# A macaron block on one core: flag 2's bank and place, tile 2's norm, the loads, the orders and one warm-up product changed

## The chip, the cores and the metric

The kernel runs on one core of one Trainium2 chip. The metric is device microseconds of one execution, as the median of several; three runs of the kernel before gave 368.39, 368.41 and 369.13 us. The engines are TensorE (PE, matrix products into PSUM), VectorE (DVE), ScalarE (ACT), GpSimd (POOL) and SyncE (SP), which here only issues DMAs. Each engine runs its own instructions in order and waits on semaphores for the others.

## The reference

The input is 16 x 256 tokens of 128 features. A feed-forward block, an attention-like block with cumulative sums, and the same feed-forward block again are added to it, each behind a layer norm:

```python
def _L0_ffn_ref(x, w1_w, w1_s, w2_w, w2_s, h1_w, h1_s, h2_w, h2_s, w3_w, w3_s):
    h = silu(_tlin(x, w1_w, w1_s)) * _tlin(x, w2_w, w2_s)     # 128 -> 512
    h = gelu(_tlin(h, h1_w, h1_s))                            # 512 -> 512
    h = gelu(_tlin(h, h2_w, h2_s))                            # 512 -> 512
    return _tlin(h, w3_w, w3_s)                               # 512 -> 128

def _L0_attn_ref(...):
    h = layer_norm(x, gamma, beta)
    keys = h @ Wk.T + bk;  values = h @ Wv.T + bv;  key_att = keys @ Wka.T + bka
    w = exp(key_att / sqrt(128));  w = w / cumsum(w, axis=1)
    return cumsum(w * keys, axis=1) * values

x = x + 0.5 * ffn(layernorm(x));  x = x + attn(layernorm(x));  x = x + 0.5 * ffn(layernorm(x))
```

`_tlin(x, w, s)` is a product with a matrix of -1, 0 and 1, scaled by `s`.

## The kernel before

The 4096 tokens are eight tiles of 512. Each goes through the first feed-forward pass as tile 0 to 7, through attention (`a0` to `a7`) and through the second pass as tile 8 to 15. Activations stand transposed, features on partitions. Every activation is split into a high part (`act_hi`, cast to fp32r) and a low part (`act_lo`, the rest), so that two fast products per weight block replace one slow one.

One tile of the feed-forward pass is `p1.0` to `p1.3` (first layer, gate and up, four blocks of four products), `p2.0` to `p2.3` and `p3.0` to `p3.3` (second and third layer, eight products each) and `p4` (eight products). ACT does `tanh`, `gelu` and the high parts (`high1`, `high2`, `high3`), DVE `gate`, `up`, the low parts (`low1` to `low3`) and the final addition `dt`. The orders are written out by hand: `START` (lines 27 to 42) for the time before the loop, `SECOND_LAYER` (45 to 49) for tile 0's second layer, and `STEPS` (50 to 185), one string per engine and step. In a string, `p2.1` is block 1 of the tile due at this step, `2:t` the stage `t` of tile 2, `a0:u` of attention tile 0. `t` is the split of the normalised input into `xn_hi` (ACT) and `xn_lo` (DVE).

There are two ways for a tile's norm. The first three tiles (`BY_PE`, line 188) are normalised in rows: DVE takes statistics (`stats`, `aggr`, `veps`), POOL makes `rstd` and `nmr`, ACT writes `z`, PE transposes it (`t`, lines 787 to 798). All other tiles go over POOL: it aggregates the statistics (`aggregate`, 534 to 553), SP parks mean and root in DRAM (`park`, 488 to 495, rows<-pair) and loads them back widened over all partitions (`wide`, 497 to 504, wide<-rows), and POOL adds and multiplies (`xn.0`, `xn.1`, lines 555 to 573) on the transposed input `xt_sb`.

The weights are proved to fit the fast format while the kernel runs: their low bits are reduced to a flag (`bits:...`, `flag:raise`), PE sums it over the partitions into one PSUM element (`flag:sum`, line 751), DVE casts it (`flag:copy`, 1024), and PE loads it into a register and branches to the fast or the general program (lines 854 to 860). There are three such flags and branches: flag 1 ahead of tile 0's first layer, flag 2 ahead of its second layer, flag 3 ahead of all the rest. Flag 2 is summed in `y_ps`, which `p1.3` of tile 0 writes later, so `p1.3` waits for the flag (line 682). Flag 3 is summed in `xt_ps`.

SP's loads (471 to 486) are in one queue: weights and tile 1 first, then, once `w3` and `h2` are down, all of `x` from tile 2 on (1536 KB), four attention weights and all of `xt` (2048 KB). Before its first real product PE multiplies ones (`warm_up`, 842): four products at once, two after the first variance, one after `rstd`.

## Time and profile before

| | us |
| --- | --- |
| median of three runs | 368.41 |
| profiled execution, its own time | 368.15 |
| its span, first to last instruction | 366.4 |
| PE busy | 359.3 |
| DVE busy | 316.2 |
| ACT busy | 283.1 |
| POOL busy | 163.3 |

What follows is read from one profiled execution. Times in it count from the span's start. PE's matrix products overlap: a product of 512 columns is shown with 0.39 us, while the next one starts 0.23 us after it, so the distance between starts is what counts.

### The profile page before, as it was taken

Reading aid. Unit: us, or ns where it says so; the run is one execution under the profiler, and the core shown is the slowest. Engines: PE = TensorE matmul, PEld = TensorE weight load, DVE = VectorE, ACT = ScalarE, POOL = GpSimd, SP = SyncE. Lnnn points to the kernel's source line nnn. Section 1 sums busy time; section 2 is a strip of 40 time slices with the busy share of each in tenths; the row PEclk is TensorE's granted clock in tenths of the full one; section 3 lists DMA queues with packets and bytes.
Section 4 is the critical chain, followed back from the end, with each engine's and each line's share of the span. In section 5 each row is a group of like instructions: output and inputs, shape, how many; then the busy total and the mean of one; then the engine's idle time right before and its main releaser. Section 6 shows DMA issues by size and latency. Waiting matters only on the chain.

```text
span 366.4 us, 5194 instructions
## 1 busy us (share of the span) xinstructions
PE 359.3 (98%) x1578; PEld 285.1 (78%) x1578; DVE 316.2 (86%) x550; ACT 283.1 (77%) x465; POOL 163.3 (45%) x251
## 2 busy tenths in 40 slices
PE   7999999999999999999999999999999999999996
PEld 2678888787877777788778787787778777888885
DVE  5999688999989998889899989998899799857642
ACT  4998777987777879776887968877897697686763
POOL 3553344649045565812685545652573740530000
PEclk9999999999999999999999999999999999999999
DMA  7770103030100301300222012012022020040001
GB/s 245 270 294 4 54 3 107 8 110 9 58 2 0 86 29 36 83 0 2 59 59 59 1 59 59 0 59 86 0 59 88 2 86 2 4 111 2 1 30 63
DMA packets 16256, 20.94 MB, mean 57 GB/s; under 512 B 7008, under 2 KB 8288, under 8 KB 15968
## 3 DMA queue, kind: packets, MB, share of 16 engines
q1 hardware_dynamic: 15504, 19.75, 18.2%
q10 hardware_dynamic: 720, 0.80, 0.7%
q8 instruction: 16, 0.26, 0.3%
q14 instruction: 16, 0.13, 0.1%
HBM read 18.36 MB, written 2.18 MB: 56 GB/s over the span
## 4 chain that ended last, share of the span: by engine, by line
PE 96%; DVE 2%; issue 1%; ACT 1%; POOL 0%; POOLq 0%; ACTq 0%
PE hid_ps L643 62%; PE gate_ps L643 8%; PE y_ps L643 8%; PE up_ps L643 7%; PE y_ps L662 2%; PE xt_ps L829 2%; PE xt_ps L833 2%; PE xt_ps L836 2%; PE y_ps L843 1%; PE gate_ps L707 1%; PE up_ps L707 1%; DVE gate L1070 0%; PE xt_ps L643 0%; DVE xt_sb L1142 0%; PE xt_ps L656 0%
## 5 line engine op out<-in xcount | busy, mean ns | idle before, releaser
L643 PE MATMUL hid_ps<-act_hi,hi_h 128*128 128x512 f32 x480 | 193.3, 403 | 0.0
L643 PE MATMUL hid_ps<-act_lo,hi_h 128*128 128x512 f32 x480 | 186.7, 389 | 0.0
L1092 DVE TENSOR_TENSOR act_lo<-full,act_hi 128x512 fp32r<-128x512 f32 x185 | 132.8, 742 | 23.6 <-ACT act_hi L909 20.6
L902 ACT ACTIVATE full<-hid_ps,vec 128x512 f32<-128x512 f32 x123 | 84.1, 687 | 57.2 <-PE hid_ps L643 51.7
L643 PEld LDWEIGHTS hid_ps<-act_hi,hi_h 128*128 128x128 f32 x480 | 90.3, 188 | 22.8 <-issue 2.6
L643 PEld LDWEIGHTS hid_ps<-act_lo,hi_h 128*128 128x128 f32 x480 | 90.2, 188 | 21.3 <-issue 2.6
L909 ACT ACTIVATE act_hi<-full 128x512 fp32r<-128x512 f32 x127 | 78.6, 628 | 1.6
L567 POOL TENSOR_TENSOR xnt<-xt_sb,wide 128x512 f32<-128x512 f32 x21 | 29.4, 1400 | 45.8 <-DMA wide<-rows 45.8
L885 ACT ACTIVATE tanh<-gate_ps,s_half 128x512 f32<-128x512 f32 x60 | 40.4, 680 | 7.4 <-PE gate_ps L643 7.3
L1070 DVE SCALAR_TENSOR_TENSOR gate<-tanh,gate_ps 128x512 f32<-128x512 f32 x60 | 40.3, 674 | 6.5 <-ACT tanh L885 6.4
L1082 DVE SCALAR_TENSOR_TENSOR full<-up_ps,s_half,gate 128x512 f32<-128x512 f32 x60 | 44.1, 741 | 1.1
L890 ACT ACTIVATE act_hi<-full 128x512 fp32r<-128x512 f32 x60 | 36.9, 625 | 1.9 <-DVE full L1082 1.7
L573 POOL TENSOR_TENSOR xnt<-xnt,wide 128x512 f32<-128x512 f32 x21 | 30.0, 1428 | 3.2 <-POOL xnt L567 0.4
L622 POOL TENSOR_TENSOR xt_sb<-xt_sb,adelta 128x512 f32<-128x512 f32 x8 | 12.3, 1532 | 42.7 <-DVE adelta L1174 42.7
L540 POOL TENSOR_TENSOR pair_diff<-stats 128x4 f32<-128x4 f32 x21 | 8.2, 388 | 44.2 <-DVE stats L1040 44.2
L1158 DVE RECIPROCAL rcsum<-csum 128x256 f32<-128x256 f32 x16 | 27.8, 1740 | 0.0
L553 POOL TENSOR_TENSOR pair<-veps,half 128x4 f32<-128x4 f32 x21 | 26.1, 1244 | 3.3 <-POOL veps L550 0.4
L643 PE MATMUL gate_ps<-xn_hi,hi_w 128*128 128x512 f32 x59 | 25.1, 425 | 0.3 <-ACT full L902 0.3
L643 PE MATMUL y_ps<-act_hi,hi_w 128*128 128x512 f32 x60 | 23.8, 396 | 0.0
L643 PE MATMUL y_ps<-act_lo,hi_w 128*128 128x512 f32 x60 | 23.4, 390 | 0.0
L643 PE MATMUL gate_ps<-xn_lo,hi_w 128*128 128x512 f32 x59 | 23.0, 391 | 0.0
L643 PE MATMUL up_ps<-xn_hi,hi_w 128*128 128x512 f32 x59 | 23.0, 390 | 0.0
(170 smaller groups left out, 440.3 us busy)
## 6 DMA issues: line engine op xcount, KB each, us to landing
wide<-rows SPq DMA_DIRECT2D x42, 256.0 KB, 3.7
xt_sb<-xt SPq DMA_DIRECT2D x1, 2048.0 KB, 10.6
out<-xt_sb SPq DMA_DIRECT2D x7, 256.0 KB, 4.0
x_sb<-x SPq DMA_DIRECT2D x1, 1536.0 KB, 6.8
raw_h<-h2t SPq DMA_DIRECT2D x4, 256.0 KB, 7.1
raw_h<-h1t SPq DMA_DIRECT2D x2, 256.0 KB, 6.1
rows<-pair SPq DMA_DIRECT2D x21, 4.0 KB, 2.2
raw_w<-w2t ACTq DMA_DIRECT2D x1, 256.0 KB, 4.0
```

The lines of the kernel that those rows point to most:

```text
L553: eng.tensor_tensor(pair_b[q][:, 1, :], veps[:, :], half[:, :], ALU.pow).then_inc(s_pow, 1)
L567: eng.tensor_tensor(xnt_b[i][:, :], xt_tile(t), wide_b[i][:, 0:TOK], ALU.add).then_inc(s_centred, 1)
L573: eng.tensor_tensor(xnt_b[i][:, :], xnt_b[i][:, :], wide_b[i][:, TOK:2 * TOK], ALU.mult).then_inc(s_xn, 1)
L643: mm = eng.matmul(ps, w, a, start=(first and n == 0), stop=(last and n == len(seq_) - 1))
L885: eng.activation(tanh_b[m % 2][:, :], gate_home(T, m)[:, :], ACT.Tanh, scale=s1_half[:, m:m + 1]).then_inc(s_tanh, 1)
L890: eng.activation(act_hi[first_act(T)][:, m, :], full1[m % 2][:, :], ACT.Copy).then_inc(s_hi[1], 1)
L902: eng.activation(full23[m % 2][:, :], home23(n, T, m)[:, :], ACT.Gelu, scale=col("sh1" if n == 2 else "sh2", m)).then_inc(s_gelu[n], 1)
L909: eng.activation(act_hi[n][:, m, :], full23[m % 2][:, :], ACT.Copy).then_inc(s_hi[n], 1)
L1070: eng.scalar_tensor_tensor(gate_b[m % 2][:, :], tanh_b[m % 2][:, :], 1.0, gate_home(T, m)[:, :], ALU.add, ALU.mult).then_inc(s_gate, 1)
L1082: eng.scalar_tensor_tensor(full1[m % 2][:, :], up_home(T, m)[:, :], s12_half[:, m:m + 1], gate_b[m % 2][:, :], ALU.mult, ALU.mult).then_in ...
L1092: eng.tensor_tensor(act_lo[a][:, m, :], full[m % 2][:, :], act_hi[a][:, m, :].bitcast(F32), ALU.subtract).then_inc(s_lo[n], 1)
L1158: eng.reciprocal(rcsum[:, b], csum[:, b]).then_inc(s_rc, 1)
```

## The change

- `WARM_UP` loses its last product, the one that waited for `rstd`.
- Flag 2 is summed in `gate_ps[0]` after `p1.3` of tile 0, and waits for the first `gate` to have read that bank; `p1.3` no longer waits for the flag.
- Tile 2's norm goes over POOL, with `stats_2` before tile 0's last `low1`. It gets loads of its own: tile 2 of `x` and of `xt`, ahead of the other tiles. The rest of `xt` is two loads.
- All orders are written anew.

```diff
-WARM_UP = (4, 2, 1)
+WARM_UP = (4, 2)
 START:
-        "p1.0 p1.1 flag:sum2 p1.2 p1.3",
+        "p1.0 p1.1 p1.2 p1.3 flag:sum2",
...
-    "p2ahi.0 p2ahi.1 p2ahi.2 p2ahi.3 p2alo.1 p2alo.3 p2bhi.3 p2alo.0 p2alo.2 p2bhi.0 p2bhi.2 t p2blo.0 p2bhi.1 "
+    "p2ahi.2 p2ahi.1 p2ahi.3 p2alo.2 p2alo.3 p2alo.1 p2ahi.0 p2bhi.0 p2bhi.1 p2bhi.2 p2alo.0 p2blo.1 p2blo.0 "
...
 STEPS["PE"], first two rows:
-        "p1.2 p1.3 fold p3.0 p3.1",
-        "t 0:p3.2 p1.0 0:p3.3 p2.0 p1.1 p2.1 p2.2 p2.3 p4 p1.2 p1.3 a0:u p3.0 p3.1 p3.2 p3.3",
+        "p1.2 fold p1.3 p3.0 p3.1 p3.2 p3.3",
+        "p1.0 p1.1 p2.0 p2.1 p4 p2.2 p2.3 p1.2 a0:u p1.3 p3.0 p3.1 p3.2 p3.3",
...
-BY_PE = (0, 1, 2)
-AGGREGATE = 3
+BY_PE = (0, 1)
+AGGREGATE = 2
...
-            return (hid_ps[0], y_ps, xt_ps)[part - 1][0:1, 0:1]
+            return (hid_ps[0], gate_ps[0], xt_ps)[part - 1][0:1, 0:1]
...
-            xload(2, NT, s_xr)
+            xload(2, 3, s_x2t)
+            eng.dma_start(xt_tile(2), xt[:, 2 * TOK:3 * TOK]).then_inc(s_xt2, 16)
+            xload(3, NT, s_xr)
...
-            eng.dma_start(xt_sb[:, :], xt).then_inc(s_xt, 16)
+            eng.dma_start(xt_sb[:, 0:2 * TOK], xt[:, 0:2 * TOK]).then_inc(s_xt, 16)
+            eng.dma_start(xt_sb[:, 3 * TOK:], xt[:, 3 * TOK:]).then_inc(s_xt, 16)
...
+                elif t == 2:
+                    eng.wait_ge(s_xt2, 16)
                 elif t < NT:
-                    eng.wait_ge(s_xt, 16)
+                    eng.wait_ge(s_xt, 32)
...
-                if (T, m) in ((0, 3), (1, 1)):
-                    eng.wait_ge(s_flag, T + 2)
+                if (T, m) == (1, 1):
+                    eng.wait_ge(s_flag, 3)
...
                 if part == 2:
-                    eng.wait_ge(s_xlo_half, 2)
+                    eng.wait_ge(s_gate, 1)
```

PE, tile 0's first layer and flag 2 (`inexact` is the flag, `hi_w1` and `hi_w2` the gate's and the up's weights). Before:

```order
L643 MATMUL up_ps1<-xn_lo,hi_w2 128x512
L764 MATMUL y_ps<-ones,inexact 1x1 [waits s_xlo_half,s_inexact]
L643 MATMUL hid_ps0<-xn_hi,hi_w1 128x512
L643 MATMUL hid_ps0<-xn_lo,hi_w1 128x512
L643 MATMUL hid_ps1<-xn_hi,hi_w2 128x512
L643 MATMUL hid_ps1<-xn_lo,hi_w2 128x512
L643 MATMUL y_ps<-xn_hi,hi_w1 128x512 [waits s_flag]
```

The same place on PE after the change:

```order
L649 MATMUL up_ps1<-xn_lo,hi_w2 128x512
L649 MATMUL hid_ps0<-xn_hi,hi_w1 128x512
L649 MATMUL hid_ps0<-xn_lo,hi_w1 128x512
L649 MATMUL hid_ps1<-xn_hi,hi_w2 128x512
L649 MATMUL hid_ps1<-xn_lo,hi_w2 128x512
L649 MATMUL y_ps<-xn_hi,hi_w1 128x512
L649 MATMUL y_ps<-xn_lo,hi_w1 128x512
L649 MATMUL xt_ps<-xn_hi,hi_w2 128x512
L649 MATMUL xt_ps<-xn_lo,hi_w2 128x512
L770 MATMUL gate_ps0<-ones,inexact 1x1 [waits s_gate,s_inexact]
```

The flag's sum moved behind all products of the first layer, and none of these waits for the flag any more.

DVE, from flag 1's cast to the second `up` (`full1_1`), before:

```order
L1027 CAST flag_i<-hid_ps0 1x1 [waits s_fps]
L1012 TENSOR_REDUCE bits<-raw_h1 128x1 [waits s_h1_0]
L1122 TENSOR_TENSOR xn_lo<-xt_ps,xn_hi 128x256 [waits s_xhi_half]
...
L1022 TENSOR_REDUCE inexact<-bits 128x1 [waits s_bits_w2,s_bits_w1,s_bits_h1]
L1045 MEMSET fence 128x1 [waits s_bn]
L1047 BN_AGGR mv<-stats_1 128x2 x4
L1070 SCALAR_TENSOR_TENSOR gate_0<-tanh_0,gate_ps0 128x512 [waits s_tanh]
L1054 TENSOR_SCALAR neg_mean<-mv 128x4 [waits s_nmr,s_mv]
L1055 TENSOR_SCALAR veps<-mv 128x4
L1027 CAST flag_i<-y_ps 1x1 [waits s_fps]
L1082 SCALAR_TENSOR_TENSOR full1_0<-up_ps0,s12_half,gate_0 128x512 [waits s_p1,s_gate,s_scaled]
L1070 SCALAR_TENSOR_TENSOR gate_1<-tanh_1,gate_ps1 128x512 [waits s_tanh]
```

DVE, the same place after:

```order
L1124 TENSOR_TENSOR xn_lo<-y_ps,xn_hi 128x256 [waits s_xhi_half]
L1014 TENSOR_REDUCE bits<-raw_h1 128x1 [waits s_h1_0]
...
L1072 SCALAR_TENSOR_TENSOR gate_0<-tanh_0,gate_ps0 128x512 [waits s_tanh]
L1042 BN_STATS stats_1<-x_sb 128x6 [waits s_x1t]
L1042 BN_STATS stats_1<-x_sb 128x6 x3
L1084 SCALAR_TENSOR_TENSOR full1_0<-up_ps0,s12_half,gate_0 128x512 [waits s_p1,s_gate,s_scaled]
L1047 MEMSET fence 128x1 [waits s_bn]
L1049 BN_AGGR mv<-stats_1 128x2 x4
L1024 TENSOR_REDUCE inexact<-bits 128x1 [waits s_bits_w2,s_bits_w1,s_bits_h1]
L1072 SCALAR_TENSOR_TENSOR gate_1<-tanh_1,gate_ps1 128x512 [waits s_tanh]
L1029 CAST flag_i<-gate_ps0 1x1 [waits s_fps]
```

The reduction of `h1`'s first part moved behind `xn_lo`, and flag 2's cast behind the second gate.

SP, its queue after the first loads: the last load of `x`, the attention weights, `xt`, and tile 3's and then attention tile 0's parked rows, before:

```order
L470 DMA x_sb<-x 128x3072 [waits s_w3,s_h2_3]
L485 DMA wk<-wkt 128x128
...
L486 DMA xt_sb<-xt 128x4096
L495 DMA rows<-pair_0 128x2x4 [waits s_pow]
L503 DMA wide_0<-rows 128x512 [waits s_parked_0]
```

SP after the change, where `pair_0` is tile 2's:

```order
L473 DMA x_sb<-x 128x512 [waits s_w3,s_h2_3]
L487 DMA xt_sb<-xt 128x512
L473 DMA x_sb<-x 128x2560
L490 DMA wk<-wkt 128x128
...
L491 DMA xt_sb<-xt 128x1024
L492 DMA xt_sb<-xt 128x2560
L501 DMA rows<-pair_0 128x2x4 [waits s_pow]
L509 DMA wide_0<-rows 128x512 [waits s_parked_0]
```

The loads are cut so that tile 2 comes first, and tile 2's parked rows now follow the last piece of `xt` in the same queue.

## Rows read from the trace of the kernel before

**Rows 1.** Busy time by stretch: PE, PEld, DVE, ACT, POOL; clock, DMA share, GB/s.
```profile
27.00:360.00 333.00, 332.99 (x1457) 267.77 (x1458) 292.77 (x479) 261.31 (x421) 150.08 (x226) 1.00 0.15 40
```
**Rows 2.** Timeline of PE, 30 to 34 us: start, us, what.
```profile
30.63 0.60 PE L656 MATMUL xt_ps<-ident,z 128*128 128x128 f32 x4
...
31.30 0.39 PE L643 MATMUL hid_ps<-act_lo,hi_h 128*128 128x512 f32 x1
...
33.14 0.39 PE L643 MATMUL gate_ps<-xn_lo,hi_w 128*128 128x512 f32 x1
```
**Rows 3.** Chain that ended last, in order of time: start, us, what.
```profile
56.26 7.25 PE hid_ps L643 x32
```
**Rows 4.** Timeline, the start, PE and DVE; last, the line of the flag's loads.
```profile
2.12 3.15 PE L843 MATMUL y_ps<-ones 128*1 128x256 f32 x7 [2.12 <-POOL ident L530]
...
6.65 0.81 PE L843 MATMUL y_ps<-ones 128*1 128x256 f32 x3
...
7.30 0.24 PE L756 MATMUL hid_ps<-ones,bits 128*1 128x1 f32 x4
...
7.58 0.15 DVE L1027 CAST flag_i<-hid_ps 1x1 int32<-1x1 f32 x1 [0.30 <-PE hid_ps L756]
...
8.69 0.36 PE L678 MATMUL gate_ps<-xn_hi,hi_w 128*128 128x256 f32 x1 [0.56 <-ACT xn_hi L968]
...
L856 PEldq TENSOR_LOAD <-flag_i x3: 304/307/492, 7.8 to 22.8; - x3
```
**Rows 5.** Timeline, 6 to 14 us, DVE, and PE's first product of the second layer.
```profile
7.65 0.67 DVE L1012 TENSOR_REDUCE bits<-raw_h 128x1 f32<-128x512 uint16 x1
...
8.70 0.41 DVE L1122 TENSOR_TENSOR xn_lo<-y_ps,xn_hi 128x256 fp32r<-128x256 f32 x1
...
12.04 0.14 DVE L1027 CAST flag_i<-y_ps 1x1 int32<-1x1 f32 x1
...
13.46 0.75 DVE L1082 SCALAR_TENSOR_TENSOR full<-up_ps,s_half,gate 128x512 f32<-128x512 f32 x1
...
13.64 0.47 PE L707 MATMUL gate_ps<-act_hi,hi_h 128*128 128x512 f32 x1 [0.22 <-ACT act_hi L890]
```
**Rows 6.** Timeline of PE, 20 to 28 us: third stage's first product, and `p3.0`.
```profile
24.12 0.39 PE L643 MATMUL gate_ps<-xn_hi,hi_w 128*128 128x512 f32 x1
...
26.86 0.49 PE L643 MATMUL hid_ps<-act_hi,hi_h 128*128 128x512 f32 x1
```
**Rows 7.** Timeline of POOL, 12 to 45 us: casts of `h2`, tile 3's norm.
```profile
18.27 2.76 POOL L584 CAST hi_h<-raw_h 128x512 fp32r<-128x512 f32 x4
...
30.02 0.21 POOL L540 TENSOR_TENSOR pair_diff<-stats 128x4 f32<-128x4 f32 x1 [4.71 <-DVE stats L1040]
...
38.73 1.29 POOL L567 TENSOR_TENSOR xnt<-xt_sb,wide 128x512 f32<-128x512 f32 x1 [5.62 <-DMA wide<-rows]
40.17 1.56 POOL L573 TENSOR_TENSOR xnt<-xnt,wide 128x512 f32<-128x512 f32 x1
```
**Rows 8.** Timeline of SP's issues, 13 to 40 us: start and time of issuing.
```profile
16.05 0.45 SPq L486 DMA_DIRECT2D xt_sb<-xt  x1
...
34.73 0.34 SPq L503 DMA_DIRECT2D wide<-rows  x1
```
**Rows 9.** Lines of tiles `xn_hi` and `wide`: min/median/max in ns; last, landing in us.
```profile
L961 ACT ACTIVATE xn_hi<-xnt x13: 616/626/642, 50.5 to 328.7; 128x512 fp32r<-128x512 f32 x13
...
L1127 DVE TENSOR_TENSOR xn_lo<-xnt,xn_hi x13: 675/683/1124, 51.4 to 329.3; 128x512 fp32r<-128x512 f32 x13
...
DMA to landing us min/median/max: 3.1/3.7/4.8
```
**Rows 10.** DMA issues from 13 to 36 us: KB each, median us to landing.
```profile
xt_sb<-xt SPq DMA_DIRECT2D x1, 2048.0 KB, 10.6
...
wk<-wkt SPq DMA_DIRECT2D x1, 64.0 KB, 6.0
...
rows<-pair SPq DMA_DIRECT2D x1, 4.0 KB, 1.6
```

62 lines of the change are left out of this document (27 added, 35 removed), and 178 rows, old and new, of tables (SECOND_LAYER, START, STEPS).

## The prediction

> **What bounds the kernel now.** First the table of stretches: from 27 us to 360 us PE (TensorE) is busy for 332.99 of 333 us, at a granted clock of 1.00, with VectorE (DVE) busy for 293 us and ScalarE (ACT) for 261 [rows 1]. There the time is PE's own work, and no other engine's saving is worth anything. What an order can give or lose lies in the first 35 us, where PE is still fed by single results. After 360 us the last tile's chain runs; its PE order is the same in the changed kernel, so I count nothing for it. The sum is therefore the time at which one fixed point of PE's stream is reached, before and after; all behind it moves along. I take the low product of tile 2's first gate (`p1.0` of tile 2), with the whole of tile 0's third layer done. Before, that product starts at 33.14 [rows 2], with `0:p3.3` (8 products) still to come; 32 products take 7.25 in the steady stream, 0.227 each [rows 3]. So the point lies at 33.14 + 8 x 0.227 = 34.95.
>
> **Start, to the first product.** One warm-up product goes. It is two passes; three passes span 6.65 to 7.30, 0.22 each [rows 4], so the flag sum behind it starts 0.43 sooner, at 6.87. Its inputs are there (DVE's reductions of `w1`, `w2` end before 6.41, where `z` begins). DVE's flag cast then waits for the three `z` pieces instead of PE and starts near 7.2 instead of 7.58 [rows 4], so PE's first product comes at about 8.3 instead of 8.69. The transposes move by the same 0.43, and so do ACT's `xn_hi` and DVE's `xn_lo`: the second `xn_lo` starts at 8.27 instead of 8.70 [rows 5].
>
> **Flag 2.** Before, PE's sum of flag 2 stands between `p1.1` and `p1.2` and makes them wait for DVE. That stall goes: all products of tile 0's first layer run through and end near 12.2. But the second branch needs the flag itself. On DVE, from the second `xn_lo` (8.70) to the second `up` (13.46) lie 4.76 us without a gap [rows 5]. The same instructions stand there in the new order plus `bits:h1.0`, 0.67 [rows 5], which before filled the wait between the flag cast and `xn_lo` and now comes behind it. So the second `up` starts at 8.27 + 4.76 + 0.67 = 13.70, and the flag cast, which now has only the two small operations of `veps` between itself and that `up`, at about 13.45, ending at 13.6. Before, the cast ended at 12.18 [rows 5]. From a cast's end to PE's first product took 0.96 for flag 1 (7.73 to 8.69, `TENSOR_LOAD` and branch within it) [rows 4]; a part of this may be the wait for `xn_hi`, so 0.96 is the upper bound and 0.5, the longest load of the flag alone (492 ns) [rows 4], the lower. I take 0.85, nearest to the one whole passage seen. The second layer then begins at 13.6 + 0.85 = 14.45 instead of 13.64 [rows 5]: **+0.8**, with PE idle some 2.2 us before it, and the first `act_hi` is no later than that by my count of ACT (about 13.9).
>
> **Second stage.** Before it ran from 13.64 to 24.12 [rows 5, 6], 10.48 for 40 products of 0.23, four transposes (0.44) and a flag sum (0.2): 9.85 of work and 0.6 of waits. In the new order each operand is ready before its turn, since PE comes later to the same chain; I leave 0.1 for waits. End: 14.45 + 9.95 = 24.4, **+0.3**. The third flag is ready about 0.5 before PE's last four products there, so its branch is hidden as it is now, where the stream goes on at 24.12 without a pause.
>
> **Third stage to `p3.0`.** Before: 24.12 to 26.86 [rows 6], 2.74 for 8 products (1.82) and the four short ones of `fold`, the rest a wait for the fourth `gelu2`. Now `fold` stands ahead of `p1.3`, and it writes `xt_ps`, which DVE's `1:gate.1` must have read; that gate starts only after `flag:copy3`, `up.0`, `low2.0`, `low2.1`, near 25.05, and ends near 25.7. `p1.3` then waits a little for the fourth `gelu2`. I get 27.2 for `p3.0`: **+0.35**, bounds +0.0 and +0.8.
>
> **Tile 2's transposes** leave PE. They cost 31.30 - 30.63 - 0.23 = **-0.44** [rows 2]. Then 32 products of `p3` and the high product: 27.2 + 33 x 0.227 = 34.7. Against 34.95 that is -0.25: PE alone would gain a quarter of a microsecond.
>
> **Tile 2's norm on GpSimd (POOL).** This is the new wait. The pieces, as tile 3 has them now: the aggregation from 30.02 [rows 7] to the parking's issue, 34.73 - 1.6 = 33.13; the parking 1.6 [rows 8, 10]; the widening to the first addition 38.73 - 34.73 = 4.0; addition and multiplication 38.73 to 41.73 = 3.0 [rows 7, 8]; then `xn_hi` on ACT 0.63 and `xn_lo` on DVE 0.68 [rows 9]. POOL starts it after `low1` and three casts of `h2`: before, the casts began at 18.27 and all four took 2.76 [rows 7]; now the first comes at about 18.35 and the norm at 20.5, and the roots are done at 23.6. Parked at once, the rows would be back at 25.2. But the queue on SyncE (SP) is full: the load of `xt`, issued at 16.05, lands after 10.6, at 26.65 [rows 8, 10]. Does it hold the parking? `wk`, 64 KB, issued right behind the 1536 KB of `x`, took 6.0, while the pair of 256 KB each on an idle queue took 4.0 and the 4 KB of the parking 1.6 [rows 7, 8, 10]. So yes: I take 26.65 (the bounds are 25.2 and 27.5). Then 4.0 + 3.0 gives 33.65, 0.63 + 0.68 and some 0.15 of hand-over 35.1. The cost of the split loads themselves is nothing: the same bytes, three more issues.
>
> The Trainium skill, page "DMA: Bandwidth & Descriptors", section "Queues, rings and completion order", says that each DMA engine consumes a ring in order and that a semaphore's increment lands only after every earlier write of that engine. By this rule the parking can't be told done before the last piece of `xt` is down, which speaks against the change; the trace agrees with it (6.0 for `wk`). Without the rule the sum would be that of the first rival.
>
> **Sum.** The point is reached at the later of 34.7 (PE) and 35.1 (tile 2's normalised rows): 35.1 against 34.95, **+0.15**. `2:t` stands on DVE ahead of `1:up.3`, which `p1.1` needs: ready at 35.8, PE there at 35.8, nothing. On ACT `2:t` holds `gelu3.2`, which `p2.0` needs at 36.7 and has at 35.6. The rest has the same work; tile 3's rows, next in the chain, are ready near 46 and wanted near 48. The profiled execution took 368.15 (span 366.4), 0.26 below the median: 368.3 there, 368.55 for the median; I say **368.5**. A measurement here can tell about 0.2% (0.74 us) from no change.
>
> **The rivals.** (1) *The loads don't hold the parking*: it lands at 25.2, the rows are ready at 33.7, PE decides: -0.25, 368.15. Against it stands `wk`. (2) *Clearly faster*: as (1), and DVE's `bits:h1.0` costs nothing and the third stage has no new wait (0.35 less): -0.25 - 0.67 - 0.35 = -1.3, 367.1; half of it 367.6. For it speaks that my hand count of DVE has some 0.3 of play at each step. (3) *Slower, by the norm's chain*: the mechanism is PE waiting at `p1.0` of tile 2. It decides from 34.7 on and makes the kernel measurably slower once the rows come after 35.7. The widening's transfers took up to 4.8 where I have 4.0 [rows 9], and the queue may end at 27.5: 0.8 + 0.85 = 1.65 at worst, rows at 36.75 and +1.8, 370.2; the middle of this case is rows at 36.2, +1.25: 369.65. (4) *Slower, by the clock*: The warm-up passes are spaced 0.42 (six from 2.12 to 4.63) and later 0.22 [rows 4], that is the level of 1.2 and of 2.4 GHz, though the granted clock reads 1.00 throughout. The new stop of 2.2 us before the second layer is longer than any in PE's stream before. If the clock falls there, the slow passes at the start, some 4.2 us from 2.12 on [rows 4], are the nearest price: half of them lost, 2.1, less the 0.4 of slack: +1.85, 370.25. The Trainium skill, page "TensorE: Matmul & The Clock Gate", Part 1, has the clock halved when PE has been idle; whether this stop is enough no row here shows. (5) *A new wait in the steady stretch*: DVE's 88% [rows 1] leaves little play for the new orders: +0.3 to +1.
>
> **Chances.** Forecast 0.41; (1) 0.17; (2) 0.19; (3) 0.12; (4) 0.05; (5) 0.06. Within 0.2%: 0.41 + 0.17 = 0.58, less 0.01 for a small (5) that I count as slower: 0.57. Faster by over 0.2%: 0.19. Slower: 0.24. The range from 367.4 to 369.9 leaves out the better half of (2), 0.09, and the worst of (3) and (4), 0.09.
>
> **What would show it.** PE's second layer begins at 14.45, not 13.64; flag 2's cast is at 13.4; `p3.0` at 27.2; no transposes of tile 2 on PE; POOL's first `xnt` at about 30.7; PE waits about 0.4 before tile 2's low gate product, released by `xn_hi` and `xn_lo`; no other wait until 360. The prediction is wrong if the second layer starts before 14 (the DVE count), if the parked rows land before 26 (the queue), or if PE's products after 14 us are spaced 0.43 apart (the clock).

## The result, and the profile after

The changed kernel takes 369.72 us in the median of 20 executions (368.65 to 373.43); the kernel before, timed beside it, 368.46. The ratio is 1.004, with a 95% interval of 1.0029 to 1.0051 (the quotient of the two medians is 1.0034; the ratios given here and below are not exactly these quotients): the change makes the kernel slower by 0.4%, 1.26 us in the medians. The forecast was 368.5 and no measurable change; the time lies in its range, but the kernel did become slower. Two executions far above all others, 518.52 us of the kernel before here and 402.87 us of `b_nowarm2` below, count in no ratio and in none of the counts below. The profiled execution of the changed kernel took 369.33 us, its span is 367.5 us.

The points of the prediction in the two profiled executions (us from the span's start; the two rows marked * are starts of products, read below or in the rows of before; 34.95 is the prediction's sum, not a row):

| | before | forecast | after |
| --- | --- | --- | --- |
| first product of the first layer | 8.69 | 8.3 | 8.62 |
| cast of flag 2 | 12.04 | 13.45 | 13.62 |
| first product of the second layer | 13.64 | 14.45 | 14.40 |
| third stage, first product | 24.12 | 24.4 | 24.58 |
| `p3.0` of tile 0 | 26.86 | 27.2 | 27.30 |
| parked rows of tile 2 are down | - | 26.65 | 27.46 |
| fixed point, low product of tile 2's first gate * | 34.95 | 35.1 | 35.40 |
| first of the last four products * | 361.82 | 361.97 | 363.36 |

PE's timeline of the changed kernel from the start to `p3.0` (start, us, what; in brackets the idle time before it and its releaser), to be held against [rows 4, 5, 6]:

```profile
3.77 3.62 PE L847 MATMUL y_ps<-ones 128*1 128x256 f32 x8
7.19 0.28 PE L762 MATMUL hid_ps<-ones,bits 128*1 128x1 f32 x4
...
8.62 0.36 PE L684 MATMUL gate_ps<-xn_hi,hi_w 128*128 128x256 f32 x1 [0.45 <-ACT xn_hi L970]
...
12.23 0.39 PE L649 MATMUL xt_ps<-xn_lo,hi_w 128*128 128x512 f32 x1
13.16 0.19 PE L770 MATMUL gate_ps<-ones,inexact 128*1 128x1 f32 x2 [0.55 <-DVE inexact L1024]
14.40 0.47 PE L713 MATMUL gate_ps<-act_hi,hi_h 128*128 128x512 f32 x1 [1.04 <-ACT act_hi L892]
...
27.30 0.39 PE L649 MATMUL hid_ps<-act_hi,hi_h 128*128 128x512 f32 x1
```

Eight warm-up passes take 3.42 us from 3.77 to the flag sum at 7.19, 0.43 each to the last, where before the last three were spaced 0.22. So without the product the flag sum begins 0.11 us sooner (7.30 before) and not 0.43. All products of the first layer run through to 12.62, and then PE stands for 1.78 us, but for the flag's sum.

ACT and DVE in the stop, the same execution, show what it waited for:

```profile
12.20 0.64 ACT L916 ACTIVATE csum<-raw_h 128x512 f32<-128x512 uint16 x1
12.80 0.63 ACT L916 ACTIVATE rcsum<-raw_h 128x512 f32<-128x512 uint16 x1
...
13.42 0.63 ACT L892 ACTIVATE act_hi<-full 128x512 fp32r<-128x512 f32 x1
```
```profile
12.95 0.16 DVE L1024 TENSOR_REDUCE inexact<-bits 128x1 f32<-128x6 f32 x1
13.03 0.68 DVE L1072 SCALAR_TENSOR_TENSOR gate<-tanh,gate_ps 128x512 f32<-128x512 f32 x1
13.62 0.14 DVE L1029 CAST flag_i<-gate_ps 1x1 int32<-1x1 f32 x1
```

ACT's pass over `h1.3` (`csum` is only its scratch output) and the read of its sum end at 12.92. DVE's reduction to flag 2 (`inexact`) begins right behind them, and the pass over `h2.0` keeps the first `act_hi` until 13.42. The second layer needs both, the flag and `act_hi`.

POOL, SP and PE on tile 2's norm, which has no counterpart before ([rows 7 to 10] show tile 3's):

```profile
30.67 1.67 POOL L575 TENSOR_TENSOR xnt<-xt_sb,wide 128x512 f32<-128x512 f32 x1 [6.76 <-DMA wide<-rows]
32.49 1.29 POOL L581 TENSOR_TENSOR xnt<-xnt,wide 128x512 f32<-128x512 f32 x1
```
```profile
23.37 0.39 SPq L501 DMA_DIRECT2D rows<-pair  x1
27.48 0.34 SPq L509 DMA_DIRECT2D wide<-rows  x1
```
```profile
34.65 0.47 PE L649 MATMUL gate_ps<-xn_hi,hi_w 128*128 128x512 f32 x1
35.40 0.50 PE L649 MATMUL gate_ps<-xn_lo,hi_w 128*128 128x512 f32 x1 [0.28 <-DVE xn_lo L1129]
35.73 0.40 PE L649 MATMUL up_ps<-xn_hi,hi_w 128*128 128x512 f32 x1
```

POOL's norm begins at 20.69. The parking, issued at 23.37, is down at 27.46, 0.18 us behind the last load of `xt`. That load was issued at 16.85 (before, at 16.05, with fewer loads ahead of it) and was down 10.4 us later.

PE's wait is the one that was forecast, a little longer: its distances there are 0.32, 0.75 and 0.33 where 0.23 is normal. Behind it the prediction had PE's stream unchanged. It is not. The table of stretches (us, busy time and instructions of PE, PEld, DVE, ACT, POOL; clock, DMA share, GB/s) shows three stretches in which PE is not full, where [rows 1] had 0.01 us of idle time in all:

```profile
34.00:60.00 26.00, 25.72 (x115) 20.80 (x114) 21.84 (x42) 20.47 (x35) 14.88 (x28) 1.00 0.16 42
...
135.00:138.00 3.00, 2.95 (x13) 1.81 (x12) 2.42 (x4) 2.33 (x5) 1.07 (x1) 1.00 0.00 0
...
331.00:334.00 3.00, 2.85 (x13) 2.05 (x12) 2.02 (x4) 1.48 (x3) 0.12 (x1) 1.00 0.00 0
```

Between 60 and 135 and between 138 and 331 us PE is full. The busy time hides most of a wait, since the product ahead of it is shown with 0.39 us; the distances between starts tell it. At 136 us two distances exceed 0.227 by 0.21 and 0.11, at 332 us by 0.31 and 0.11. The first of the last four products (L747 before, L753 after), one line of each kernel's timeline:

```profile
361.82 0.60 PE L747 MATMUL gate_ps<-full,raw_w 128*128 128x256 f32 x2
```
```profile
363.36 0.60 PE L753 MATMUL gate_ps<-full,raw_w 128*128 128x256 f32 x2
```

So 1.54 us are lost up to there: 0.45 at the fixed point and 0.11 behind it (35.40 to 35.73), 0.32 at 136 us, 0.42 at 332 us, and 0.24 in small differences all along. Some 0.2 of these 0.24 belong to the new steps and not to a wait: `a_best` and its two filled variants below have the same steps and no wait of this kind, and still need 327.06, 327.00 and 327.17 us from the fixed point to these products, where the kernel before needs 326.87. (The span is 1.1 longer and not 1.5, because the last stores of this execution landed 0.4 sooner after their issue, in 2.1 us and not 2.5.)

### The profile page after: what moved, and what is told of

Same layout as the page of the kernel before. It is cut to its first block, busy times and chain, and to the rows that moved or that the text cites. A ratio compares the mean times of both kernels' runs of the same rounds, so it can differ in the third digit from the quotient of the medians.

```text
span 367.5 us, 5188 instructions
## 1 busy us (share of the span) xinstructions
PE 359.6 (98%) x1572; PEld 284.8 (77%) x1572; DVE 316.2 (86%) x543; ACT 281.7 (77%) x461; POOL 171.7 (47%) x259
## 4 chain that ended last, share of the span: by engine, by line
PE 84%; DVE 4%; DMA 4%; POOL 4%; issue 2%; ACT 1%; POOLq 0%; ACTq 0%; DVEq 0%; SPq 0%
PE hid_ps L649 54%; PE gate_ps L649 7%; PE y_ps L649 7%; PE up_ps L649 7%; PE y_ps L668 2%; DMA wide<-rows 2%; DMA rows<-pair 2%; PE xt_ps L833 2%; PE xt_ps L840 2%; PE xt_ps L837 2%; PE y_ps L847 1%; POOL xnt L575 1%; DVE act_lo L1094 1%; DVE gate L1072 1%; POOL hi_h L592 1%
## 5 line engine op out<-in xcount | busy, mean ns | idle before, releaser
L575 POOL TENSOR_TENSOR xnt<-xt_sb,wide 128x512 f32<-128x512 f32 x22 | 32.6, 1484 | 44.7 <-DMA wide<-rows 44.7
L581 POOL TENSOR_TENSOR xnt<-xnt,wide 128x512 f32<-128x512 f32 x22 | 31.0, 1407 | 3.0 <-POOL xnt L575 0.4
L649 PE MATMUL gate_ps<-xn_hi,hi_w 128*128 128x512 f32 x59 | 26.0, 440 | 0.0
L649 PE MATMUL gate_ps<-xn_lo,hi_w 128*128 128x512 f32 x59 | 23.3, 394 | 0.4 <-DVE xn_lo L1129 0.3
L649 PE MATMUL y_ps<-act_hi,hi_w 128*128 128x512 f32 x60 | 23.3, 389 | 0.0
L649 PE MATMUL y_ps<-act_lo,hi_w 128*128 128x512 f32 x60 | 23.3, 389 | 0.0
L649 PE MATMUL up_ps<-xn_lo,hi_w 128*128 128x512 f32 x59 | 23.1, 391 | 0.0
## 6 DMA issues: line engine op xcount, KB each, us to landing
xt_sb<-xt SPq DMA_DIRECT2D x1, 1280.0 KB, 10.4
```

The costliest lines, as they stand in the source:

```text
L575: eng.tensor_tensor(xnt_b[i][:, :], xt_tile(t), wide_b[i][:, 0:TOK], ALU.add).then_inc(s_centred, 1)
L581: eng.tensor_tensor(xnt_b[i][:, :], xnt_b[i][:, :], wide_b[i][:, TOK:2 * TOK], ALU.mult).then_inc(s_xn, 1)
L649: mm = eng.matmul(ps, w, a, start=(first and n == 0), stop=(last and n == len(seq_) - 1))
```

## The experiments

All runs are compared with the kernel before, timed beside them on the same chip. To tell where time goes, each profiled execution is read at two places: the *fixed point*, and the *stretch* from it to the first of the last four products (326.87 before, 327.96 after). Both vary from one execution to the next: the changed kernel and five runs with its orders from the second stage on (`a_warm`, `a_busy`, `a_stop`, `a_stop2`, `a_stop_fill`) have stretches of 327.54 to 327.96, and where their clock stays full, the fixed point lies between 34.98 and 35.98. A difference of 0.4 us between two single profiles therefore shows nothing by itself; a wait that is always there or never does.

### Warm-up product put back

```diff
-WARM_UP = (4, 2)
+WARM_UP = (4, 2, 1)
```

> The changed kernel with the warm-up product of TensorE put back (waiting for the root, as before); all else stays changed. Theory A (the removed product costs and gives nothing that reaches the end): in the profile of the changed kernel the two passes that went did not bring the flag sum forward by 0.43 us, because the passes kept their 0.43 spacing up to 7.19. With the product back the first product of the first layer starts between 8.55 and 8.75 (8.63 without it), and the low product of tile 2's first gate stays at 35.3 to 35.5, since tile 2's norm on GpSimd decides it. Time within 0.2 us of the changed kernel. Rival (the missing product leaves TensorE at the low clock for longer and this is carried to the end): 0.4 us or more faster than the changed kernel, and everything behind 8.6 us earlier by as much.

369.70 us, ratio 1.0035 (1.0023 to 1.0048). The first product comes at 9.16, the fixed point at 35.25, the last products at 363.13. The time doesn't move, as theory A has it, but the first product was expected at 8.75 at the latest: the warm-up passes kept their wide distance, 0.42 or 0.43 us, up to 7.21 us here. PE, half a microsecond late from there on, comes to the fixed point without a wait; its lateness, and rows that are down 0.5 sooner here (26.97), have taken the place of the wait.

### The xt loads behind tile 2's widening

```diff
-            eng.dma_start(xt_sb[:, 0:2 * TOK], xt[:, 0:2 * TOK]).then_inc(s_xt, 16)
-            eng.dma_start(xt_sb[:, 3 * TOK:], xt[:, 3 * TOK:]).then_inc(s_xt, 16)
...
                     wide("ffn" if stage == "wide" else "att", t)
+                    if (stage, t) == ("wide", 2):
+                        eng.dma_start(xt_sb[:, 0:2 * TOK], xt[:, 0:2 * TOK]).then_inc(s_xt, 16)
+                        eng.dma_start(xt_sb[:, 3 * TOK:], xt[:, 3 * TOK:]).then_inc(s_xt, 16)
```

> The changed kernel, with the two loads of xt (tiles 0 and 1, and tiles 3 to 11) issued by SyncE behind tile 2's parking and widening instead of ahead of them. Theory A (these loads stand in the queue ahead of the parking and hold it): the parking, issued near 23.4, lands within 1.6 to 2.2 us, before 25.8 (27.46 in the changed kernel), GpSimd's first addition of tile 2 starts near 29 (30.67), and the low product of tile 2's first gate starts when TensorE gets there, at 34.8 instead of 35.40; the time falls by 0.6 us against the changed kernel, to about 369.1. Rival B (the parking waits for the load of x, which is still in the queue, or for something else than xt): it still lands after 26.5, and the time stays within 0.2 us. Rival C (the widening then shares its transfers with the xt loads and is late): the parking is early but the first addition is still after 30.

368.83 us, ratio 1.0019 (1.0005 to 1.0033). PE has no wait at the fixed point any more:

```profile
34.48 0.39 PE L650 MATMUL gate_ps<-xn_hi,hi_w 128*128 128x512 f32 x1
34.71 0.39 PE L650 MATMUL gate_ps<-xn_lo,hi_w 128*128 128x512 f32 x1
```

34.71 is the time at which the prediction had PE arrive (34.7), and the last products are 0.94 sooner. The time gains too: the nine executions with a full clock have a median of 368.80, the eight such executions of `a_warm` and `a_stores` on the same chip 369.55. But the parking itself, with nothing large ahead of it, still took 3.3 us, issued at 23.30:

```profile
26.67 0.34 SPq L507 DMA_DIRECT2D wide<-rows  x1
```

Theory A expected it down before 25.8. The DMA queues of this execution from 23.3 to 27.6 us (packets, MB, share of 16 engines) show what moved:

```profile
q1 hardware_dynamic: 272, 0.00, 3.8%
q8 instruction: 1, 0.02, 1.9%
```

One packet of instructions, 16 KB, went at 24.23 for 1.32 us; 240 of the parking's 256 packets of 16 bytes went in the microsecond from 24 us, the last 16 from 25.54 to 25.69, beginning as the instruction packet ends (25.55). `a_mend` and `a_mend_pool` (below) show the same: the last 16 packets begin within 0.02 us of the end of the instruction packet, and the parking takes 3.0 and 3.3 us. In `a_best` and its two filled variants the parking is issued by 22.93, the instruction packet goes only at 25.6 or later, and the parking takes 1.6 us in all three, as in [rows 10]. So the likely reading is that the last 16 packets stood behind the instructions on one of the 16 DMA engines; the trace doesn't name the engine of a packet, and no run was made to test it.

With the loads ahead of it, the parking landed 0.18 to 0.31 us behind the last load of `xt` in all nine profiled executions of that kind: the loads do hold it. But that load itself landed sooner or later, so the parking took 3.1 to 5.5 us there and 3.0 to 3.3 with the loads behind it; in `a_pool`, with the loads ahead, the rows were down as early as here (26.66) and PE had no wait either. So theory A is right in the mechanism; its 1.6 us without the loads is wrong, and the 0.8 us between 27.46 and 26.65 are those of two single executions.

### The last widening ahead of the stores

```diff
-        "park 9:store 10:store 11:store wide store",
+        "park wide 9:store 10:store 11:store store",
```

> The changed kernel, with SyncE's last widening issued ahead of the stores of tiles 9 to 11 instead of behind them. Theory A (the 0.42 us that TensorE waits near 332.3 come from these stores, which stand between the parking and the widening): the parking of the last norm lands 1.6 us after its issue (2.84 in the changed kernel), the widening's transfers take under 3.8 us (4.2), TensorE does not wait there, and the last store is issued 0.42 us sooner relative to the product of the same place at 320 us: time 0.4 us under the changed kernel, 369.3. Rival (DVE's statistics for that norm, which come 0.9 us later than in the kernel before, decide): a wait of more than 0.2 us stays there.

PE's wait at 332 us is gone: 332.25 and 332.48 are the starts of the high and the low product of tile 15's first gate. It is a wait that belongs to this order: between 0.11 and 0.73 us were lost there in all nine profiled executions with the three stores ahead of the widening, and at most 0.04 in the six with the widening ahead. The stretch is 327.58 instead of 327.96. SP's issues in the changed kernel and here:

```profile
321.29 0.37 SPq L501 DMA_DIRECT2D rows<-pair  x1
321.71 1.44 SPq L519 DMA_DIRECT2D out<-xt_sb  x3
324.18 0.33 SPq L509 DMA_DIRECT2D wide<-rows  x1
```
```profile
321.46 0.37 SPq L501 DMA_DIRECT2D rows<-pair  x1
324.09 0.32 SPq L509 DMA_DIRECT2D wide<-rows  x1
```

The parking itself was hardly quicker (2.63 us, 2.89 in the changed kernel, expected 1.6); what the stores held were mainly the widening's own 512 KB: from its issue to POOL's first addition 3.59 us instead of 4.20. The time, 370.02 us, ratio 1.0044 (1.0029 to 1.0059) from five executions, does not show the gain; 0.4 us is within what five executions leave open.

### The old start in the changed kernel

```diff
-        "p1.0 p1.1 p1.2 p1.3 flag:sum2",
+        "p1.0 p1.1 flag:sum2 p1.2 p1.3",
```

and the `START` strings of ACT and DVE and flag 2's bank of the kernel before.

> The changed kernel, with the start of the kernel before on TensorE, VectorE and ScalarE (flag 2 summed in its old bank between the second and the third product group of the first layer, the old order of casts and flag work); the second and third stage, GpSimd's norm of tile 2 and all later orders stay changed. Theory A (the start is hidden behind tile 2's norm on GpSimd): the second layer begins at 13.6 to 13.8 instead of 14.40 and the third layer 0.5 to 0.8 us sooner, but the low product of tile 2's first gate still starts at 35.3 to 35.5, with TensorE waiting about 1.2 us there; time within 0.2 us of the changed kernel. Rival (the later second layer is what reaches the end): 0.5 to 0.8 us faster than the changed kernel, 369.0 or less, and the low product starts before 35.0.

372.15 us, ratio 1.0101 (1.0084 to 1.0117): both expectations fail. The second layer begins at 13.31, but PE stands for 2.8 us in the third stage, and behind that stop the granted clock falls (0.70 from 27 to 29 us, 0.50 from 29 to 31). The trace names no releaser for the stop (`issue`); that it comes of mixing two orders is my reading.

```profile
26.89 0.47 PE L649 MATMUL gate_ps<-xn_hi,hi_w 128*128 128x512 f32 x1 [2.77 <-issue]
...
29.65 0.63 PE L649 MATMUL up_ps<-xn_hi,hi_w 128*128 128x512 f32 x1
30.08 0.63 PE L649 MATMUL up_ps<-xn_lo,hi_w 128*128 128x512 f32 x1
```

The run says nothing on whether the start is hidden. It gave the clue to the next question: a mean granted clock of 0.994 or 0.995 over the execution, in all four of its executions. With the start of before (the kernel before itself, and later `b_nowarm` and `b_flag`) no execution whose clock is on record read below 0.998; of the changed kernel 3 in 20 read 0.993 to 0.995, and these took 370.48, 370.89 and 373.43 us.

### Three mends together

The xt loads and the last widening as above, and on ACT:

```diff
-        gelu2.3 a2:t high1.0 high2.3 7:t
+        gelu2.3 a2:t high2.3 high1.0 7:t
```

> The changed kernel with three edits of its orders: the two xt loads behind tile 2's widening, the last widening ahead of the three stores, and on ScalarE the high part high2.3 of tile 5's second layer ahead of high1.0 (the low part that follows it on VectorE took 1.09 us beside GpSimd and ended 0.25 us late for TensorE at 136 us). Theory A (the three waits are what the change cost: 0.6 near 35 us, 0.3 near 136, 0.4 near 332): low product of tile 2's first gate at 34.7, no wait of TensorE over 0.1 near 136 and near 332, last four products from 361.8 to 362.1 (361.82 before, 363.36 changed), time 368.2 to 368.6, that is within 0.1% of the kernel before. Rival (a wait that goes comes back further on, since VectorE and ScalarE are the ones that are late): last four products not before 362.4, time 368.8 or more.

369.08 us, ratio 1.0006 (0.9993 to 1.0020). The fixed point is at 34.83, the wait at 332 us is gone, the one at 136 us is not (0.21 and 0.11, as in the changed kernel), and a new one of 0.54 stands at 260 us. The stretch is 328.03, no better than unmended, as the rival has it: waits come back further on. The time speaks for theory A all the same, within 0.1% of the kernel before, and the interval doesn't meet that of the change (from 1.0029 on). The profiled execution is slower than the median of the nine with a full clock (368.79). DVE's `act_lo` at 132.8 and 134.2 us take 1.34 and 1.61 us here, beside POOL's operations, and two at 259 and 260.5 us take 1.76 and 1.77, where the changed kernel, whose POOL began its pair 0.55 us earlier, had 0.75 and 1.36. Hence the next try, to move POOL's instruction (`a_pool`).

### Warm-up product taken out of the kernel before

```diff
-WARM_UP = (4, 2, 1)
+WARM_UP = (4, 2)
```

> The kernel before, without the last warm-up product of TensorE, and nothing else. In the pair changed kernel / changed kernel with the product back, the first product of the first layer came at 8.62 without it and at 9.16 with it. Theory A (the product delays the flag sum by its own passes, 0.43 to 0.85): first product 0.3 to 0.5 us sooner than 8.69, and the second layer and the end sooner by the same, since the kernel before has no wait on tile 2's norm that hides it: 368.0. Rival (the second layer is set by VectorE and ScalarE, and only the first product moves): the second layer stays at 13.5 to 13.7 and the time within 0.15 us of the kernel before.

> The kernel before without the last warm-up product again, to settle a difference of 0.26 us. Theory A (in the profiled execution everything from the first product on came 0.6 us sooner): ratio to the kernel before 0.998 to 0.9995, and with the earlier run beside it clearly below 1. Rival (the gain of the profiled execution was the moment at which the clock rose, which differs from one execution to the next): ratio 0.9995 to 1.0005.

368.58 us and 368.00 us, ratios 0.9993 (0.9983 to 1.0003) and 0.9991 (0.9982 to 1.0000). In the two profiled executions the second layer begins at 13.04 and at 14.09. That difference is not the product's: DVE began the statistics of the first tile of `x`, for which it had waited, at 3.91 and at 4.68, and the last four warm-up passes, spaced 0.21 in both, began at 5.53 and at 6.30. Both ratios point the same way, some 0.3 us, but neither interval excludes 1 clearly. It is the one part of the change that may gain, and no version was found that gains more.

### Flag 2's bank and place in the kernel before

```diff
-        "p1.0 p1.1 flag:sum2 p1.2 p1.3",
+        "p1.0 p1.1 p1.2 p1.3 flag:sum2",
-        ... aggr gate.0 veps flag:copy2 up.0 gate.1 ...
+        ... aggr gate.0 veps up.0 flag:copy2 gate.1 ...
-            return (hid_ps[0], y_ps, xt_ps)[part - 1][0:1, 0:1]
+            return (hid_ps[0], gate_ps[0], xt_ps)[part - 1][0:1, 0:1]
```

> The kernel before, with one part of the change alone: flag 2 is summed in the first gate bank behind the last product of tile 0's first layer, and its cast stands behind the first up on VectorE. Nothing else is changed. Theory A (the place of the sum costs only what lies between the cast and the branch): the cast is at 12.8, the second layer starts at 13.8 to 13.9 instead of 13.64, and third layer and end are within 0.2 us of the kernel before, so the 0.75 us by which the second layer is later in the changed kernel are not the bank but the new order on ScalarE, where the casts of h1.3 and h2.0 now stand between the tanh and the first act_hi. Rival (the bank is what costs): second layer at 14.2 or later, time 0.4 us or more above the kernel before.

368.70 us, ratio 1.0004 (0.9992 to 1.0015). From the first product of the first layer to that of the second it is 4.93 us (8.22 to 13.15), before 4.95, after 5.78. The bank costs nothing, not even the 0.2 that I expected; so the 0.8 must come from the new orders of ACT and DVE around it.

### The changed start in the kernel before

```diff
-        "t vec:s1 bits:h1.1 bits:h1.3 tanh.0 tanh.1 tanh.2 high1.0 tanh.3 high1.1 ... bits:h2.0 "
+        "tanh.0 tanh.1 bits:h1.1 tanh.2 bits:h1.3 bits:h2.0 high1.0 tanh.3 high1.1 ..."
```

and DVE's and PE's orders of the changed start.

> The kernel before with the changed kernel's start on TensorE, ScalarE and VectorE (flag 2 behind the first layer in the gate bank, the new order of tanh, casts, flag and act_hi up to the second layer); the warm-up product, tile 2's norm on TensorE and all later orders are those of before. Theory A (the new start alone costs, since no wait on tile 2's rows hides it here): second layer at 14.3 to 14.6, third layer 0.3 to 0.7 later than before, time 0.3 to 0.7 us above the kernel before, and a granted clock of 0.993 to 0.995 in about one execution in four. Rival (VectorE's chain through the second stage sets the third layer, whatever the start does): p3 of tile 0 within 0.15 of 26.86 and the time within 0.15 us of before wherever the clock is full.

369.81 us, ratio 1.0042 (1.0025 to 1.0058): the new start alone, without POOL's norm and with the old steps, costs as much as the whole change, twice what was expected. The second layer begins at 14.31 and the third at 28.14 (26.86 before); the low product of tile 2's first gate stands at 34.44 with eight products of `p3.3` still to come, so the fixed point is at 36.26, 1.3 later than before. PE gets one wait more that the change itself doesn't have, because the transposes of tile 1 stand earlier in the old second layer:

```profile
16.47 0.61 PE L706 MATMUL gate_ps<-act_hi,hi_h 128*128 128x512 f32 x2
17.93 0.66 PE L655 MATMUL hid_ps<-ident,z 128*128 128x128 f32 x4 [0.85 <-ACT z L931]
```

From there the stretch is 326.87, exactly that of before. So the start is no free place, and the old steps keep PE full; the losses at 136 and 332 us belong to the new steps.

### All mends, an earlier norm and a tighter start

The three mends, and:

```diff
-        "tanh.0 tanh.1 bits:h1.1 tanh.2 bits:h1.3 bits:h2.0 high1.0 tanh.3 ...
+        "bits:h1.1 tanh.0 tanh.1 bits:h1.3 tanh.2 high1.0 bits:h2.0 tanh.3 ...
-        "bits:h1.2 gate.0 stats up.0 aggr flag:raise2 gate.1 flag:copy2 veps up.1 ...
+        "bits:h1.2 gate.0 stats flag:raise2 up.0 flag:copy2 gate.1 aggr veps up.1 ...
-        "hi:h2.0 hi:h2.1 hi:h2.2 norm hi:h2.3 xn.0 xn.1",
+        "hi:h2.0 norm hi:h2.1 hi:h2.2 hi:h2.3 xn.0 xn.1",
```

> The changed kernel with the three edits of a_mend, and two more: at the start ScalarE does the bits of h1.1 ahead of the first tanh and those of h1.3 and h2.0 around high1.0, and VectorE raises flag 2 ahead of the first up; and GpSimd begins tile 2's norm after one cast of h2 instead of three. Theory A (with tile 2's rows early, the start of the second layer is what counts): flag cast at 12.9, second layer at 13.8 to 13.9 (14.40 changed), tile 2's rows ready before 33.5, low product of tile 2's first gate between 34.2 and 34.7, time 367.9 to 368.3, a little under the kernel before. Rival (the second and third stage are bound by VectorE whatever the start does): the low product stays at 34.6 to 34.8 and the time is that of a_mend.

368.52 us, ratio 1.0015 (0.9996 to 1.0034). The second layer begins at 13.66, tile 2's rows are ready on POOL at 32.84, but the fixed point is at 34.96, later than either theory has it (34.8 at most): PE waits again inside the second layer (0.64 and 0.32 over the normal distance at 13.97 and 14.83) for the operands of its next block. With tile 2's rows early and the second layer 0.74 earlier nothing is won at the fixed point. That fits the rival, by which the chain of DVE through the second stage decides; no run isolates that chain. The stretch is 327.06, without a wait at 136, 260 or 332 us. Eight executions with a full clock have a median of 368.40, below the 368.75 of the kernel before; four with a clock of 0.993 to 0.995 have one of 370.74.

### The stop before the second layer filled

```diff
+                if part == 2:
+                    eng.wait_ge(s_gate, 1)
+                    warm_up(1, gate_ps[0][0:1, 128:128 + seq])
                 eng.wait_ge(s_inexact, part - 1)
...
                            stop=True).then_inc(s_fps, 1)
+                if part == 2:
+                    eng.wait_ge(s_full1, 1)
+                    warm_up(2, up_ps[0][0:1, 0:seq])
```

The added products are of no use to the result.

> The changed kernel, with three products of the warm-up kind (128x256, of no use) on TensorE in its stop before the second layer: one into the first gate bank ahead of flag 2's sum, two into the first up bank behind it. So far a granted clock of 0.993 to 0.995 was read in 13 of 56 executions of kernels with the changed start (a_start, which stops for 3 us more, not counted) and in none of the executions of the kernel before and of b_nowarm and b_flag; they took 1 to 2 us longer. Theory A (the stop of 2.2 us before the second layer is what lets the clock fall at times): with the stop filled no execution reads below 0.9965, the spread ends near 370, and the second layer starts at 14.4 to 14.7. Rival (the clock falls for another reason, say a missing warm-up or the wait at 35 us): such executions are seen again, about 3 in 12.

> a_best with the same three products in the stop before the second layer. Its executions with a full clock had a median of 368.4, 0.3 us under the kernel before in the same call, those with a clock of 0.993 to 0.995 (4 of 12) 370.7. Theory A: no execution with the low clock, median 368.3 to 368.6 with nothing above 369.3, ratio to the kernel before 0.9985 to 1.0. Rival (the stop is not what matters to the clock): again some 3 to 4 of 12 at about 370.7.

369.58 us (1.0037; 1.0024 to 1.0050) and 368.77 us (1.0014; 1.0005 to 1.0023). None of the 18 executions has the low clock. `a_best_busy` was expected between 0.9985 and 1.0; it is a little slower than the kernel before, so the low clock is not all that separates `a_best` from a gain. (The 13 in 56 of my expectation is a miscount: with the six kernels of the changed start then run it was 16 in 67.) But `b_start`, on the same chip, had none in 6 with its stop unfilled, so the chip could have been the reason; `a_stop2` and `a_stop_fill` below answer that.

### POOL's addition moved at 136 us

```diff
-        "a2:norm norm a2:xn.0 a2:xn.1 xn.0 a1:dt xn.1",
+        "a2:norm norm a2:xn.0 a2:xn.1 xn.0 xn.1 a1:dt",
```

> The changed kernel, with one instruction of GpSimd moved: the addition that brings the first attention result into xt (a1:dt) stands behind the second half of tile 6's norm (xn.1) instead of ahead of it, as in the kernel before. In the changed kernel xn.1 (1.75 us from 134.32) ran beside VectorE's act_lo of 135.53, which took 1.09 us instead of 0.68. Theory A (VectorE's instruction is slowed by GpSimd's that runs beside it, and this makes the wait of 0.32 us at 136 us): act_lo there takes 0.67 to 0.70, no wait of TensorE over 0.05 between 135 and 138, and the last products 0.3 us sooner relative to those at 120 us, so some 0.3 us off the time. Rival (the instruction's operands come too late anyway, GpSimd has no part in it): the wait stays between 0.2 and 0.35.

My expectation is wrong in calling this the order of the kernel before: there `a1:dt` stands ahead of both `xn.0` and `xn.1`. DVE's line is as theory A wants it, 0.69 us at 135.68 instead of 1.08, and the wait at 136 us is down to 0.06. But POOL's `xn.1` now runs beside an earlier `act_lo`. DVE around 130 us in `a_xt_late`, where this order is that of the change; then DVE and POOL in `a_pool`:

```profile
130.22 1.26 DVE L1095 TENSOR_TENSOR act_lo<-full,act_hi 128x512 fp32r<-128x512 f32 x2
131.41 0.73 DVE L1177 SCALAR_TENSOR_TENSOR adelta<-xt_ps,vec,pooled 128x512 f32<-128x512 f32 x1
```
```profile
130.17 2.31 DVE L1094 TENSOR_TENSOR act_lo<-full,act_hi 128x512 fp32r<-128x512 f32 x2
132.41 0.74 DVE L1176 SCALAR_TENSOR_TENSOR adelta<-xt_ps,vec,pooled 128x512 f32<-128x512 f32 x1
```
```profile
129.85 1.49 POOL L581 TENSOR_TENSOR xnt<-xnt,wide 128x512 f32<-128x512 f32 x1
```

The same two instructions take 2.31 instead of 1.26 us, everything behind them on DVE is 1.0 later, and PE pays 0.9 at once:

```profile
132.84 0.39 PE L649 MATMUL y_ps<-act_lo,hi_w 128*128 128x512 f32 x1
133.86 0.50 PE L649 MATMUL gate_ps<-xn_hi,hi_w 128*128 128x512 f32 x1 [0.64 <-DVE full L1084]
```

370.57 us, ratio 1.0061 (1.0040 to 1.0082), of six executions, three of them with the low clock; the profiled one is the fastest of the six (368.75). So that a collision slows DVE is shown twice, at the place that theory A names and at the one to which it moved; the gain that it promised is not there.

Nor is the collision at 135.5 us enough for the wait at 136. Of the thirteen profiled executions with the changed order of POOL there, six have that wait and seven have not, and in four of the seven (`a_busy`, `a_start`, `a_stop2`, `a_stop_fill`) the same `act_lo` takes 1.09 to 1.12 us too. What parts them lies 10 us earlier. DVE in the changed kernel, and in `a_busy` (`pooled` is a cumulative sum of attention):

```profile
125.97 1.69 DVE L1094 TENSOR_TENSOR act_lo<-full,act_hi 128x512 fp32r<-128x512 f32 x1
...
128.84 2.31 DVE L1168 TENSOR_TENSOR_SCAN pooled<-ones,wgt_keys 128x256 f32<-128x256 f32 x2
```
```profile
125.54 0.77 DVE L1100 TENSOR_TENSOR act_lo<-full,act_hi 128x512 fp32r<-128x512 f32 x1
...
127.50 1.26 DVE L1174 TENSOR_TENSOR_SCAN pooled<-ones,wgt_keys 128x256 f32<-128x256 f32 x2
```

In all six executions with the wait one `act_lo` near 126 us takes 1.68 to 1.80 and one `pooled` 1.68 to 1.80, beside POOL's additions and multiplications; in the seven without it neither takes more than 0.77. In `a_busy` DVE then comes to the `act_lo` ahead of the wait 1.6 us sooner than in the changed kernel, counted from the fixed point. So the wait at 136 is the sum of several such collisions, and whether they happen differs from one execution to the next.

### The two loads' and the stores' mend with POOL's addition moved

The xt loads and the last widening as in their own runs, and `a1:dt` as in `a_pool`.

> The changed kernel with three edits: the xt loads behind tile 2's widening, the last widening ahead of the stores, and a1:dt behind xn.1 on GpSimd. Theory A (with the waits at 35, 136 and 332 us out, the changed kernel comes level with the one before): from the low product of tile 2's first gate at 34.7 to the last four products 327.1 to 327.3 us (327.96 changed, 326.87 before), these at 361.8 to 362.0, median of the executions with a full clock within 0.1% of before; executions with the low clock are still seen, one in four. Rival (another wait takes their place, as at 260 us in a_mend): 327.5 or more.

369.32 us, ratio 1.0032 (1.0015 to 1.0048). The fixed point is at 35.00, the stretch is 328.03, and the wait stands at 133 us as in `a_pool`: the rival.

### The stop made longer, and the same filled

```diff
-        ... flag:raise2 gate.1 flag:copy2 veps up.1 low1.0 ...
+        ... flag:raise2 gate.1 veps up.1 flag:copy2 low1.0 ...
```

> The changed kernel, with the cast of flag 2 on VectorE behind the second up instead of ahead of it, so that TensorE's stop before the second layer is some 0.8 us longer and nothing else is. Theory A (this stop lets the clock fall, the more often the longer it is): second layer at 15.1 to 15.3, a granted clock of 0.993 to 0.995 in half of the executions or more, and, if the profiled one is among them, products of the second layer spaced 0.43 apart for some 4 us; time 0.5 to 2 us above the changed kernel. Rival (the clock falls by chance, independent of this stop): about one execution in four as before, and the time no more than 0.5 above the changed kernel.

> a_stop again (flag 2's cast behind the second up, stop of TensorE before the second layer of some 2.9 us from the last product of the first layer), as the comparison for a_stop_fill on the same chip. Both theories: a granted clock of 0.993 to 0.995 in about half of the executions, these at about 370.9, the others at about 369.2.

> a_stop with its stop filled: one product of the warm-up kind ahead of flag 2's sum, four behind it. Theory A (the stop is the cause): no execution with a granted clock under 0.9965, median 369.2 to 369.6, second layer at 15.0 to 15.3, products after it spaced 0.23. Rival (the chip or chance): as many such executions as a_stop2 has.

> a_best_busy again, on the chip of a_stop2. Theory A (the filled stop keeps the clock): none with the low clock, ratio to the kernel before 1.0 to 1.002, so no faster version than the kernel before. Rival: 3 to 4 of 12 at about 370.7, ratio above 1.002.

`a_stop` took 370.53 us (1.0046; 1.0026 to 1.0066), and 370.71 us when run again. PE now stands from 12.5 to 15.09 us. 6 of 11 executions and then 4 of 6 read a clock of 0.993 to 0.995; in `a_stop` these six had a median of 370.91 us, the others 369.21. The profiled one is among them. Its table of stretches (columns as above):

```profile
12.00:14.00 2.00, 0.70 (x5) 0.17 (x3) 2.00 (x11) 2.00 (x7) 0.16 (x1) 1.00 0.09 20
14.00:16.00 2.00, 0.91 (x3) 0.76 (x4) 1.97 (x5) 1.91 (x4) 1.85 (x3) 0.80 1.06 279
16.00:18.00 2.00, 2.00 (x6) 1.63 (x5) 1.96 (x5) 1.56 (x5) 1.31 (x2) 0.50 0.94 364
18.00:20.00 2.00, 2.00 (x9) 1.55 (x9) 1.57 (x5) 1.10 (x3) 2.00 (x4) 0.85 0.88 310
```

The granted clock (third number from the right) falls right behind the stop to 0.50, which is 1.2 of 2.4 GHz, and is full again after 20 us; PE does 6 and 9 products from 16 to 18 and from 18 to 20 us, where it does 11 and 12 in `a_stop_fill` at the full clock. With the stop filled by five products, on the chip on which `a_stop2` had 4 of 6, none of 12 executions has it (369.68 us; 1.0039; 1.0025 to 1.0053), nor has one of 12 of `a_best_busy2` (368.80 us; 1.0016; 1.0005 to 1.0027). The first two stretches of `a_stop_fill`:

```profile
12.00:14.00 2.00, 1.98 (x12) 0.59 (x11) 2.00 (x11) 2.00 (x7) 0.18 (x1) 1.00 0.10 39
14.00:16.00 2.00, 1.83 (x9) 0.97 (x8) 1.96 (x5) 1.91 (x4) 1.85 (x3) 1.00 0.77 241
```

Over all runs the low clock came in 23 of 85 executions with the changed kernel's stop of 1.8 us or that of `a_best` (1.1 us and two short waits behind it), in 10 of 17 with the longer one, in none of 42 with a filled one, and in none on record of the kernel before, of `b_nowarm` and of `b_flag` (whose stop is 1.0 us). (`b_start`, 6 executions, had none; its stop is that of the change.) The median of the changed kernel's 17 executions with a full clock is 369.53 us, of all 20 it is 369.72: of the 1.26 us, 0.2 are the clock's.

## Why the prediction was wrong

**Flag 2: right.** The cast was expected at 13.45 and stands at 13.62, the second layer at 14.45 and 14.40. `b_flag` adds that the bank has no part in it.

**Start: the term of the warm-up was mis-sized.** At the flag sum -0.43 was forecast and -0.11 came, at the first product -0.39 and -0.07. The prediction took the last passes' spacing of before (0.22) for that of every execution. In the changed kernel's profile all passes behind the first two are spaced 0.43, in `b_nowarm` the last four are spaced 0.21, and that moves the flag sum by 0.8 (7.19 and 6.39). At the end it made no difference here: flag 2 hangs on ACT's bits.

**Second and third stage, transposes: right.** The third stage was expected at 24.4 and begins at 24.58; 27.2 was forecast for `p3.0`, 27.30 measured, and PE's own arrival at the fixed point, 34.7, is what `a_xt_late` shows (34.71).

**Norm on POOL: right in kind, short by 0.3.** The parking was down 0.8 later than my value, near the upper bound that I gave (27.5); widening and first addition (4.0 forecast) took 3.2, so `xnt` began at 30.67, where 30.65 was forecast: two errors that cancel, which is luck. The late parking is a term that the sum put at nothing ("the cost of the split loads themselves is nothing"): with the small loads ahead, the last piece of `xt` was issued 0.8 later than the load of before (16.85 and 16.05) and was down at 27.28, and the parking lands 0.18 behind it. The 0.3 at the fixed point came behind the addition: POOL's two operations took 3.11 instead of 3.0 (30.67 to 33.78), DVE's `xn_lo` 0.81 instead of 0.68, the rest is hand-over. The counterpart in the first rival, rows down at 25.2 without the loads, was wrong: a parking issued between 23.3 and 23.6 is down at 26.4 to 26.9 when the loads are out of the way. The Trainium skill, page "DMA: Bandwidth & Descriptors", section "Queues, rings and completion order", says that a semaphore's increment lands only after every earlier write of the same DMA engine; the traces agree, with the parking 0.18 to 0.31 us behind the last load in nine executions.

**"The rest of PE's stream is unchanged": this step failed.** Some 1.1 of the 1.54 us are lost behind the fixed point. I had counted the same work in it, and took from [rows 1] that PE is its own bound there. But there the operands come only just in time, and the new steps place two things at which PE then waits: three stores between the last parking and its widening (0.42, shown by `a_stores` and by the five other executions without them there), and DVE instructions beside POOL's from 126 to 136 us (0.32; the seven executions in which the first of them take their normal time have no wait there). This is rival 5, which had a chance of 0.06; its range of +0.3 to +1 is about the size, but its reason was only that DVE is 88% busy.

**The clock, rival 4: right in mechanism, wrong in dose.** I had 0.05 for it, +1.85 us, and a stop of 2.2 us, which came out as 1.8. `a_stop` and `a_stop_fill` show that it exists at this very stop, with a price of 1.7 us; it comes not in all executions or none, but in 3 of 20 of the changed kernel. It adds 0.2 to the median. The Trainium skill, page "TensorE: Matmul & The Clock Gate", Part 1, has the clock halved when PE has been idle, and the trace of `a_stop` agrees (0.50 behind a stop of 2.6 us with one small product in it).

Together: in the profiled execution 0.56 at and right behind the fixed point, 0.74 from the two waits and 0.24 from small differences, most of them the new steps' own; and 0.2 of the median from the clock. That the time lay in the range is no merit of the sum: it forecast +0.15 and got +0.45 at the fixed point, and had nothing for what came behind. Open stays what the small differences are, why the collisions near 126 us happen in one execution and not in the next, and whether the instruction packet is what lengthens the parking. I also can't say that the start is hidden: `a_best` begins the second layer 0.74 sooner and gains nothing at the fixed point, while `b_start` loses 1.3 there.

## What to carry to other kernels

A stretch in which PE is 100% busy is not one in which orders are free: the operands may come just in time, and a new order has to be gone through on every queue, SP's stores included, not only for the work that it adds. Where VectorE and GpSimd work on SBUF at once, an instruction's time depends on what runs beside it (0.68 or 1.7 us here), so moving one moves the collision; look at what it will then meet. A stop of TensorE costs more than its length in a part of the executions, and one good profile doesn't show it: read the granted clock of every execution. And a wait that one profile shows and a mend removes may have been that execution's own: profile both kernels more than once.

## What the runs showed of the hardware

- DVE's `act_lo` (two SBUF inputs, 128x512) takes 0.68 us in the median of 185 and up to 1.69 in the changed kernel, 1.77 in `a_mend` and 1.78 in the kernel before; those of 125.97 and 133.57 us in the changed kernel (1.69 and 1.34) stand beside POOL's additions and multiplications. The cumulative sum `pooled` (128x256) takes 0.66 to 0.69 us, or 1.68 to 1.80 beside them.

```profile
L1094 DVE TENSOR_TENSOR act_lo<-full,act_hi x185: 624/684/1687, 14.5 to 361.3; 128x512 fp32r<-128x512 f32 x185
```

  The Trainium skill, page "SBUF — State Buffer", section "Who interferes with whom", says that a VectorE instruction with two SBUF inputs contends with a GpSimd one that reads SBUF; `a_pool` agrees (2.31 against 1.26 us for two).
- The clock fell behind a stop of PE of 1.8 us in 3 of 20 executions of the changed kernel and in about one in four of all with such a stop or that of `a_best`, of 2.6 us in more than half, and in none of 42 in which the stop was filled with products.
- A DMA of 4 KB landed 0.18 to 0.31 us behind 1280 KB that stood ahead of it in the queue (nine executions). With no large transfer ahead it took 1.6 us in four executions, and 3.0 to 3.3 in three in which 16 KB of instructions were fetched at the same time.
- The spacing of the warm-up products drops from 0.43 to 0.21 at different moments, though the granted clock reads 1.00 throughout: the flag's sum behind the same six of them began at 6.39 (`b_nowarm`) and at 7.19 (changed kernel).
